# Encoder attention: the quotient taken between 32x32 block transposes, with Wo, the second norm and the x parts moved

## The reference

```python
q, k, v = x @ Wq[l] + bq[l], x @ Wk[l] + bk[l], x @ Wv[l] + bv[l]     # per head
a = causal_linear_attn(elu(q) + 1, elu(k) + 1, v)                      # chunks of 128 tokens
x = layer_norm(x + a @ Wo[l] + bo[l], g1[l], be1[l])                   # first norm
y = gelu(x @ W1[l] + b1[l], approximate=False) @ W2[l] + b2[l]
x = layer_norm(x + y, g2[l], be2[l])                                   # second norm
```

## Time and profile before

| what | us |
|---|---|
| three runs | 1620.52, 1620.95, 1617.94 |
| median | 1620.52 |
| the profiled execution | 1621.31 |
| its span, first to last instruction | 1619.6 |
| an ordinary encoder step, from Wo's first matmul to the next | 48.46 |
| the step of a layer's first tile (q = 0, from layer 1 on) | 50.38 |

### The profile page before, as it was taken

The page is one execution under the profiler, slowest core; times in us unless marked ns, Lnnn a source line. Parts: engine busy times, 40 slices in busy tenths (PEclk is TensorE's granted clock), DMA queues, the critical chain, the costliest instruction groups (busy, mean ns, idle before and its releaser), DMA issues.

```text
span 1619.6 us, 38530 instructions
## 1 busy us (share of the span) xinstructions
PE 1526.0 (94%) x15894; PEld 1226.1 (76%) x15894; DVE 1290.5 (80%) x2566; ACT 952.0 (59%) x1516; POOL 802.0 (50%) x580
## 2 busy tenths in 40 slices
PE   3799999999999999999999999999998999999798
PEld 3578888888888888888888888888886566666334
DVE  3777888878888888988878878888876889887456
ACT  3465556665556665566665556655544777777345
POOL 2344445545455454554555445553464466672434
PEclk8899999999999999999999999999998999999899
DMA  6120011201121011210012110102033444441001
GB/s 136 37 61 15 21 24 39 66 10 21 25 66 45 7 18 24 67 47 12 13 23 67 47 21 11 40 16 49 1 65 129 129 143 142 139 131 63 16 0 53
DMA packets 98352, 82.52 MB, mean 51 GB/s; under 512 B 23041, under 2 KB 86401, under 8 KB 98177
## 3 DMA queue, kind: packets, MB, share of 16 engines
q1 hardware_dynamic: 98176, 80.06, 18.9%
HBM read 50.78 MB, written 14.68 MB: 40 GB/s over the span
## 4 chain that ended last, share of the span: by engine, by line
PE 83%; DVE 11%; issue 2%; SPq 2%; ACT 1%; DMA 1%; POOL 0%; ACTq 0%; DVEq 0%
PE e_pr L170 10%; PE e_pr L172 8%; PE e_pr L171 8%; PE e_tr L428 6%; PE e_sc L401 6%; PE x_psO L1364 4%; PE e_tr L170 4%; PE e_tr L172 3%; PE e_tr L171 3%; PE e_sc L170 3%; PE e_sc L172 3%; PE e_sc L171 3%; PE f_bank L1902 3%; PE e_tr L438 3%; PE x_psT L1349 2%
## 5 line engine op out<-in xcount | busy, mean ns | idle before, releaser
L715 POOL TENSOR_TENSOR e_h_lo<-e_h_f,e_h_hi 128x512 fp32r<-128x512 f32 x192 | 265.4, 1386 | 282.4 <-ACT e_h_hi L557 278.4
L805 DVE TENSOR_TENSOR e_am<-e_sc,c_amask 128x1024 f32<-128x1024 f32 x192 | 225.7, 1216 | 18.9 <-PE e_sc L401 18.9
L556 ACT ACTIVATE e_h_f<-e_pr,e_h_bias 128x512 f32<-128x512 f32 x192 | 132.2, 689 | 178.0 <-PE e_pr L172 174.4
L1674 DVE TENSOR_REDUCE x_mx<-x_psS 128x4 f32<-128x1024 f32 x128 | 150.9, 1219 | 25.6 <-PE x_psS L1327 24.7
L170 PE MATMUL e_tr<-e_W_hi,e_h_hi 128*128 128x256 f32 x576 | 163.3, 283 | 8.2 <-DVE X L762 8.2
L170 PE MATMUL e_pr<-e_yT_hi,e_W_hi 128*128 128x512 f32 x384 | 169.1, 440 | 0.0
L171 PE MATMUL e_tr<-e_W_lo,e_h_hi 128*128 128x256 f32 x576 | 160.8, 279 | 0.0
L172 PE MATMUL e_tr<-e_W_hi,e_h_lo 128*128 128x256 f32 x576 | 160.7, 279 | 0.0
L172 PE MATMUL e_pr<-e_yT_hi,e_W_lo 128*128 128x512 f32 x384 | 152.9, 398 | 0.0
L171 PE MATMUL e_pr<-e_yT_lo,e_W_hi 128*128 128x512 f32 x384 | 152.3, 397 | 0.0
L1500 ACT ACTIVATE x_ex<-x_psT 128x1024 f32<-128x1024 f32 x128 | 131.0, 1023 | 26.8 <-PE x_psT L1349 22.1
(11 more groups left out here) (284 smaller groups left out, 4327.1 us busy)
## 6 DMA issues: line engine op xcount, KB each, us to landing
e_raw_m<-in_L_attn_W_dram SPq DMA_DIRECT2D x12, 1024.0 KB, 5.3
x_qs<-query_rows SPq DMA_DIRECT2D x48, 256.0 KB
e_x_raw<-e_a_tok SPq DMA_DIRECT2D x368, 32.0 KB
x_ks<-key_rows SPq DMA_DIRECT2D x48, 128.0 KB, 2.8
query_rows<-x_q_hi SPq DMA_DIRECT2D x16, 256.0 KB, 2.4
query_rows<-x_q_lo SPq DMA_DIRECT2D x16, 256.0 KB, 2.6
x_ctok<-in_ctx_dram SPq DMA_DIRECT2D x8, 256.0 KB, 3.5
x_xo<-in_x_dram SPq DMA_DIRECT2D x8, 256.0 KB, 4.0
```

The source lines that it names most:

```text
L556: act.activation(h_f[:, m % HR, :], ps_pr[m % 2][:, :], ACT.Gelu, bias=h_bias[:, m:m + 1])
L715: pool.tensor_tensor(h_lo[:, m, :], h_f[:, m % HR, :], h_hi[:, m, :].bitcast(F32), ALU.subtract).then_inc(h_lo_done, 1)
L805: dve.tensor_tensor(am[:, s % 2, c, :, :, :], ps_sc[:, :, c * 2 * P:(c + 1) * 2 * P].rearrange("p r (h n) -> p r h n", n=P), amask[:, :].u ...
L1674: dve.tensor_reduce(mx[:, N % 2, :, 0:HG].rearrange("p i (a h) -> p h a i", a=2)[:, pair], ps_s[pair][:, :, :].rearrange("p a (i j) -> p a ...
```

## The change

- `to_tokens`, `out_copy` and the transposes of `a_tok` go. `divide(s)` on DVE now takes the output from PSUM with a 32x32 block transpose of 128x512 into `o_blk`, adds eps, takes the reciprocal and multiplies from there into `a_blk` (SBUF to SBUF), and turns it back with two block transposes of 128x128 into `aT_f`. Wo's rows are loaded in the order that this leaves (8 DMAs in place of 1).
- hi and lo of the attention are made block by block: ScalarE's `out_hi(s)` and DVE's `out_lo(s)`, 128x256 each, `out_lo(s-1)` ahead of `divide(s)`. `attend(s)` waits for the block transpose of s - 1 (`o_taken`).
- Wo's product of block s follows the loop at once, with up-projections 6 and 7 behind blocks 0 and 1; `qk(0)` moves to the next step's start.
- The second norm's `centre` and `scale` (eight instructions) move to the next step, behind the first norm's `centre` and ahead of `phi`.
- `x_transpose` moves behind the y parts; both `x_hi` come at s = 2; `x_lo` moves from DVE to POOL, behind the fifth `h_lo`.
- W1's hi and lo move from the end of q = 3 to q = 0 of the next layer: hi behind ScalarE's `key_hi`, lo on POOL behind `k_lo`. W2's load follows them. The addition of `bo` moves on POOL from the step's end to behind `k_lo` (and behind W1's lo).

```diff
+    x_blk = sb_att("x_blk", [KC, NR, SB * RH])
+    o_blk, a_blk, aT_f = sb_att("o_blk", [4, NR, HP]), sb_att("a_blk", [4, NR, DH]), sb_att("aT_f", [KC, P])
@@ SP
+                if l > 0 and q == 0:
+                    sp.wait_ge(w1_lo, l + 1)
+                    load_w2(l)
...
-                    load_attn_weights(l + 1, ["Wo"], raw_o_loaded)
+                    load_wo(l + 1)
@@ TensorE
                 def attend(s):
                     if s > 0:
-                        pe.wait_ge(oT_done, SB * t + s)
+                        pe.wait_ge(o_taken, SB * t + s)
...
+                def out_weights(s):
+                    pe.wait_ge(aT_lo_done, SB * t + s + 1)
...
+                for s in range(SB):
+                    if attn:
+                        out_weights(s)
+                    if mlp and s < 2:
+                        mlp_up(6 + s)
@@ ScalarE
+                def out_hi(s):
+                    act.wait_ge(aT_tr, SB * t + s + 1)
+                    act.activation(aT_hi[:, :, blk(s)], aT_f[:, :, :], ACT.Copy).then_inc(aT_hi_done, 1)
...
+                    if q == 0 and l > 0:
+                        act.wait_ge(raw_1_loaded, 16 * (l + 1))
+                        act.wait_ge(h_full, FC * u)
+                        w_m("W1", w1_hi)
@@ GpSimd
+                elif attn:
+                    if q == 0 and l > 0:
+                        w_m("W1", w1_hi, l + 1, w1_lo)
+                    add_row(ta, rows_a["bo"], xT_tr, t + 2, bo_loaded, 16 * (la + 1), xbo_done)
...
+                        if m == 4 and following:
+                            x_lo(t + 1)
@@ VectorE
                 def divide(s):
+                    dve.wait_ge(out_full, n + 1)
...
+                    dve.transpose(o_blk[:, :, :, :].rearrange("p g b d -> p (g b d)"), taken).then_inc(o_taken, 1)
...
+                    dve.tensor_tensor(a_blk[:, :, :, :].rearrange("p g b d -> p (g b) d"), o[:, :, 0:DH],
+                                      rden[:, s, :].unsqueeze(2).broadcast_to([P, H, DH]), ALU.mult).then_inc(den_step, 1)
...
+                    for c in range(KC):
+                        v = dve.transpose(aT_f[:, c, :], a_blk[:, 2 * c:2 * c + 2].rearrange("p g b d -> p b g d"))
+                    v.then_inc(aT_tr, 1)
...
+                def out_lo(s):
+                    dve.wait_ge(aT_hi_done, SB * t + s + 1)
+                    dve.tensor_tensor(aT_lo[:, :, blk(s)], aT_f[:, :, :], aT_hi[:, :, blk(s)].bitcast(F32),
+                                      ALU.subtract).then_inc(aT_lo_done, 1)
...
-                    scale(2, u - 2, (q - 2) % NT, rows_m["be2"], range(2, SB))
+                    centre(2, u - 2, (q - 2) % NT, rows_m["g2"], ln2_rows_loaded, 32 * ((u - 2) // NT + 1))
+                    scale(2, u - 2, (q - 2) % NT, rows_m["be2"])
```

More of the change, by code:

```diff
@@ L210, in _ @@
             load_rows(0, ["bo"], rows_a, bo_loaded)
[L211 removed]
+            load_wo(0)
             load_w1(0)
@@ L307, in step @@
                     pe.wait_ge(xT_lo_done, 2 * t + 2)
[L308 to L313, removed]
+                    for j in range(KC):
+                        if prev:
+                            pe.wait_ge(gelu_done, FC * u - 1 + j)
+                        elif mlp and j == 0:
+                            pe.wait_ge(ktok_done, t)
+                        qk(j)
                     for j in range(KC, 2 * KC):
@@ L862, in step @@
                     scale(1, u, q, rows_a["be1"])
-                if following:
-                    x_transpose(t + 1, (q + 2) % NT)
+                if prev and u < final:
+                    residual(2, 0, d, last, m_full, xb2_done)
                 if u == final:
@@ L875, in step @@
                             ALU.add).then_inc(vx_done, 1)
-                if prev and u < final:
-                    residual(2, 0, d, last, m_full, xb2_done)
                 if attn:
@@ L920, in step @@
                         mask(s + 1)
-                    if prev and s == 0:
+                    if u == final and s == 0:
                         centre(2, d, last, rows_m["g2"], ln2_rows_loaded, rows)
-                    if prev and s == 2 and u < final:
-                        scale(2, d, last, rows_m["be2"], range(0, 2))
                     if attn:
+                        if s > 0:
+                            out_lo(s - 1)
                         divide(s)
@@ L933, in step @@
                     cross.encoder_stats(0)
-                if following:
-                    x_lo(t + 1)
                 if attn:
-                    for c in range(KC):
-                        dve.wait_ge(aT_hi_done, 2 * t + c + 1)
-                        low(aT_lo[:, c, :], ps_tr[c][:, :], aT_hi[:, c, :]).then_inc(aT_lo_done, 1)
+                    out_lo(SB - 1)
                 if u == final - 1:
```

130 lines of the change are left out of this document (43 added, 87 removed).

## The result

The changed kernel takes 1675.7 us (median of four, 1675.0 to 1677.0) against 1620.7 for the kernel before in the same session: 3.4% slower, a ratio of 1.034 with a 95% interval of 1.032 to 1.036. The forecast was 1654, in a range of 1606 to 1690. The profiled execution took 1675.6, its span 1673.9, 54.3 more than before.

The account below looks back on a forecast made before the run. TensorE bounds the kernel before; in the changed loop DVE's chain cancels the gain (0). Five layers add 47.5 us, less 9.6 at layer starts and 5.0 at the start: 1621.3 + 32.9 = 1654, range 1606 to 1690.

Parts of the forecast that it names:

- What TensorE loses: to_tokens and the transposes of a_tok leave TensorE: 2.74 us a step, 63 us over 23 steps.
- the layer's start: W1's lo no longer delays the first norm's rs on POOL: up to 1.92 us back at each of 5 layer starts.
- the start: At the kernel's start, x_transpose waiting for the last biases no longer holds up the values' bias: 5.0 us back.
- The chain in the loop: DVE from mask(1) to the third block transpose: 12.43 us, plus 0.7 for a collision and 1.0 in q = 2.
- What DVE and POOL do to each other: In the loop, the multiply and out_lo, now reading two SBUF inputs, wait for POOL's instructions: 0.7 us more a step.
- `bo` and W1 at the start: At a step's start POOL's bo and W1's lo meet DVE's qx_lo, delaying y transposes: 0.5, 1.4, 2.9 and 2.5 us.
- The 1.2 for `x_lo` on GpSimd: In q = 1, x_lo behind W2's four parts on POOL lets qk(0) wait another 1.2 us.
- The sum: A layer loses 9.5 us and regains 1.9; over 5 layers, with 5.0 back at the start, 32.9 us slower.
- The chain without collisions: Rival: the loop's multiply and out_lo fall beside POOL's instructions, under 0.7 us a step lost, time 1590; chance 0.14.
- TensorE stays the bound: Rival: all of the 2.74 us a step saved on TensorE counts, time 1544; chance 0.03.
- Eps waits too: Rival: den (eps) in the loop's chain also waits for POOL, 0.8 us a step, 18 us more, 1672; chance 0.20.

Follow-up runs that it names:

- e5: Changed kernel with GpSimd's addition of bo moved beside DVE's phi and W1's lo at a layer's start moved behind the four qx_lo: 1628.2 us.
- e3: Changed kernel with 12 extra matmuls ahead of attend(3) in each step with an MLP, to fill TensorE's wait there: 1685.6 us.
- e1: Changed kernel with GpSimd's h_lo replaced by a memset of its output to zero: 1644.2 us.
- e12: Changed kernel with e5's moves, divide's multiply on GpSimd, out_hi one block later and GpSimd's queue reordered: 1602.9 us.
- e6: Changed kernel with divide's multiply given to GpSimd, block transposes alternating between two tiles, transposes back and out_lo one block later: 1703.6 us.

## Why the prediction was right in its sign and short in its size

It said 33 slower; it was 55. By its own steps:

- **What TensorE loses, the layer's start, the start** held: the two kinds of transposes are gone, and the start gave 5.75 for 5.0, in part by luck: 3.1 of it stood ahead of the first mask, the other 2.7 behind it, where the transposes are gone, which the forecast had not counted in that step. The layer's start gives less than the 1.92 a layer: 1.48 where it was tried alone.
- **The chain in the loop** held to the tenth (14.16 against 14.13 in q = 2, 13.0 to 13.1 against 13.13 elsewhere), with its prices: 0.70 for 0.69, 0.292 for 0.29. So did the wait: 3.2 behind q = 2's weight parts, 2.1 to 2.2 in the other steps, plus 0.34 to 0.40 at the scores; forecast 2.7 and 3.7.
- **What DVE and POOL do to each other** held as a mechanism. The multiply, 424 to 425 ns for 96 of 96 before, became 424 to 1406; the trace agrees with the rule of the Trainium skill's page "SBUF — State Buffer" (section "Who interferes with whom") that the prediction cites. One collision a step was priced; 59 of 96 multiplies collided, 1.8 us a step for 0.7. Those of blocks 2 and 3 fall behind the third block transpose and are harmless to `attend(3)`, which is why the chain still fits; that DVE's later work pays for them is argued, not tried alone.
- **`bo` and W1 at the start.** Forecast 0.5 + 1.4 + 2.9 + 2.5 = 7.3 us a layer ahead of the y transposes; measured, in the layer from 461.8 to 667.0, 1.93 + 2.11 + 1.04 + 1.03 = 6.1. e5 confirms the cause. The 1.2 for `x_lo` on GpSimd did not come.
- **The sum** is the step that failed. Step by step, the layer from 461.8 to 667.0 takes 205.2 us where it took 195.7: 9.4 more, forecast 9.5 - 1.9 = 7.6. On TensorE's account three terms are off. First, TensorE was priced at full clock: the mean granted clock is 0.97 in each of those four steps, and 1.4 us a step, about 32 us over 23 steps, is in its account and not in the forecast. e3 and the row of the fourth block transpose speak against this as the root. DVE's account seems the better one, and there the missing pieces would be the 1.1 us a step of multiplies above the forecast and eps; no run takes these away alone. Second, the losses were taken 5 times, where 23 steps are 5.75 layers: 0.75 x 9.5 = 7 us. Third, nothing was forecast for what follows the last Wo products: 434.45 us in place of 430.37, 4.1 more, with the clock at 0.86 in the first 20. Against these the waits themselves were set some 3 us a layer too high (8.5 + 4 x 2.7 + 1.0 = 20.3 for 6.1 + 11.1 = 17.2). Counted on TensorE: - 5.9 (the start, to the end of the first Wo products) + 5.75 x (17.2 of waits - 10.96 of transposes gone) - 5 x 1.9 + 32 + 4.1 = 57, against 54.3 measured.
- **The rivals.** *The chain without collisions* is out: 59 multiplies collided, and more than 0.7 a step was lost. e1 and e5 take 31.6 and 47.5 us off, and either is still slower than the kernel before; if the two added up, which was not run, the change would be at 1597. That the collisions alone decide the sign is therefore not shown. *TensorE stays the bound* is out. *Eps waits too* was given 0.20 and came true in part: `den` is at 695 ns at worst where it was at 176, and its 96 take 29.9 us for 16.4 before, 13.5 more. The Trainium skill's page "SBUF — State Buffer" (section "Who interferes with whom") says that such an operation can wait for GpSimd; the trace agrees, and 16 elements were enough. But the rival put the wait into the chain to the third block transpose, and there it is not: of the 48 eps of blocks 0 and 1 none is long (0.17 to 0.18), the 35 long ones are in blocks 2 and 3. That its 1672 is nearest to the result is luck.

## What to carry to other kernels

In this kernel, moving work from TensorE to a second engine would have paid only if the second engine's chain between two of TensorE's waits had stayed shorter than TensorE's own: add that chain up instruction by instruction before looking at busy shares. When an operand moves from PSUM to SBUF, look at what GpSimd runs beside it, and look at all of DVE's instructions with two tiles of SBUF, not only the new ones: placing `bo` beside DVE's PSUM readers and W1's lo behind `qx_lo` was worth 47 us together, with no work saved; in e12 GpSimd's parts met the norm. And the order of a queue ranks with the work in it: six instructions of a norm cost 55 us more in one place than in another, and one 0.6 us multiply behind 9 us of parts nobody was waiting for cost more than the collisions it avoided (e6, 28 us slower). Last, read a gain by its steps: most of e12's 1% lies in the start and the step behind it.

## What was not expected of the hardware

- The clock at the 1.2 GHz level behind waits of 3.2 us in an engine that was busy for 46.8 of 51.4 us: such waits can cost more in TensorE's account than their own length (1.94 + 0.79 + 0.59 for what took 1.4 less). The wait's length alone does not decide it: `attend(3)` took 1.94 behind one wait of 3.22 us and 1.08 behind another of the same length.
- A four-element DVE sum between two tiles of SBUF took 2.16 us beside GpSimd's `bo`, and eps on 16 elements up to 0.70: the wait goes by GpSimd's instruction, not by the size of DVE's.
- In e1 a GpSimd memset, which reads nothing, left the two-input multiply at its 0.42 in 40 overlaps. Eps did wait: the one long eps that met only a memset took 0.52 for 0.17, and five that met a W2 part and then a memset took 0.99 to 1.00, to the memset's end. The two kinds of DVE instruction do not mind the same things.
